# Silu on ScalarE with the router's weight as its scale, and one-hot vectors compared in one instruction

## The chip, the cores and the metric

One core of one Trainium2 chip runs the whole program. The metric is the device time of one execution in microseconds. Five engines work side by side and meet through semaphores: TensorE (PE, with its weight loads shown apart as PEld), VectorE (DVE), ScalarE (ACT), GpSimd (POOL) and SyncE (SP), which here only issues DMAs.

## The reference

The input `x` is 2 sequences of 2048 tokens with 256 channels. After a layer norm, a recurrent branch (RWKV-7 time mixing, 4 heads of 64) gives `s`, and a feed-forward branch gives `g`. The change is in the second branch and in where it meets the first:

```
logits = xn @ gate_w.T + gate_b                # 8 experts
scores = softmax(logits);  top_v, top_i = top_k(scores, 2)
val_sum = top_v.sum(-1)                        # the router's weight
for e in range(8):
    gate  = (top_i == e).sum(-1) * val_sum     # 0 or val_sum
    inter = xn @ wi.T + bi + (xn @ lora_A[e].T) @ lora_B[e].T
    out  += gate * (relu(inter) @ wo.T + bo)
g = silu(out)
x = x + s * g
```

Both chosen experts have the same weight `val_sum`. So `out` is `val_sum * y1`, where `y1` is the sum of the two experts' outputs, `(relu1 + relu2) @ wo.T + 2 * bo`.

## The kernel before

The work goes in 16 tiles of 128 tokens of each sequence (two chunks `g` of 64 tokens of each sequence, so 128 partitions times `G = 2`). A tile passes through three stages, and each of the 18 steps of the program (loop at L1495) works on three tiles at once: `front` of one tile (norm, router, mixing, projections), `rec` of the tile before it (the recurrence and the experts) and `post` of the tile before that (output projection, gate, residual). Step 1 has `front` alone, step 2 `front` and `rec`, steps 3 to 16 all three, step 17 `rec` and `post`, step 18 `post` alone.

The order on every engine is written out by hand in one function `tile` for each engine (PE L578, ACT L913, POOL L1056, DVE L1386). Each engine runs its list in order, and an instruction that waits for a semaphore holds up all that is behind it on that engine. `till(name, n)` gives the count to wait for. At the start of a step each engine waits for `act_end`, `pool_end` and `dve_end` of the step before; in the middle steps TensorE first does `base(0)`.

What the change touches:

- The router's one-hot vectors on VectorE: `first_expert` (L1172) and `second_expert` (L1185) end with one compare for each chunk, 128x8 each (L1183, L1195). `gate_sum` (L1205) leaves the router's weight in `vsum`, one number per token.
- The expert sum: `down` on TensorE (L275) adds into the bank `FB`; `y1_` (L1272) reads it on VectorE and adds the bias; `ypre` (L1277) multiplies by `vsum`, one instruction per chunk.
- The gate, one step later: `ysg_` on ScalarE (L850) takes Sigmoid of `y1`; `fgate_` on VectorE (L1282) multiplies the two; `o_read` (L1286) multiplies the output projection by `fgate`.

ScalarE evaluates its functions from a table, and a row ACT_TABLE_LOAD stands in its list wherever the next function needs another one. In the second half of a step its list runs: `kraw_` (two copies out of a bank, L819 and L820, once TensorE's `wk_B` is there), `sig_` (Sigmoid of the decay, L806), `copy_blocks` (four copies into `tinvT`, L872), `zt_e` (L848), `hg` (Tanh, L796), `inv_last` (L878), `p_out` (L883), `keys_out` (L887), `relu(2, 3)` (L762), `sa_out` (L893).

On TensorE the same stretch is `wk_B` (L360, L362), `inv_off(4)`, `rec_p(0)`, `top_x`, `zt_` (L289, the transposes of `zz`), `diff(3)` (L263), `g_A` (L337, waits for `sig_done`), `top_off` (L501), `keys_to_tokens(0)` (L510), `o_` (L300, waits for `hg_done`), `rec_sa(0)` (L542, waits for `p_done`). The bank that `keys_to_tokens(0)` writes is the one that `zt_e` reads, so TensorE waits there for ScalarE:

```
if post:
    pe.wait_ge(*till("zt_done", 1))
...
keys_to_tokens(0)
```

Of the kernel before, what the change touches and what calls it, by code (L numbers as in the profile page):

```python
# [28 lines left out]
G = 2  # L29
# [15 lines left out]
PER = dict(xn_done=G, xm_done=2, dx_done=3, mixt_done=2, miu_mm=3, sig_done=2, agate_done=2, xmask_done=2, e8_done=2 * G,  # L45
           oh1_done=G, oh2_done=G, dg2_done=2, v_done=3, down_mm=PAIRS, var_done=G, ypre_done=G,
           g_mm=LEVELS, g_stored=LEVELS, ar_scaled=LEVELS, bk0_scaled=LEVELS, bk1_scaled=LEVELS, tot_done=LEVELS,
# [7 lines left out]
       "y_done", "inc_mm", "dec_done", "state_done", "bkt_mm", "bkt_done", "yc_done", "ysq_done", "v8_done", "sd8_done",  # L55
       "bv_done", "bv_shifted", "yn_done", "zz_done", "down_mm", "y1_read", "ypre_done"}
REC |= {f"{n}_{p}_{e}" for n, e in (("z1", "mm"), ("z2", "mm"), ("relu1", "done"), ("relu2", "done"), ("hid", "done"))
        for p in range(PAIRS)}
POSTS = {"ysg_done", "fgate_done", "zt_mm", "zt_done", "o_mm", "o_read", "out_done", "out_stored"}
# [3 lines left out]
DOWN_ORDER = (1, 0, 2, 3)  # L63


def program(nc, x, par, weights, consts, out):
    ctx = ExitStack()
    with ctx:
# [60 lines left out]
        e2 = sb("e2", [128, G])  # L129
        vsum = [sb(f"vsum{i}", [128, G]) for i in range(2)]  # L130
        hit = sb("hit", [128, G, E])
# [10 lines left out]
        y1 = sb("y1", [128, G, C])  # L142
        ysg = sb("ysg", [128, G, C])
        fgate = sb("fgate", [128, G, C])
# [98 lines left out]
        def _(pe):  # L243
# [30 lines left out]

            def down(p):  # L275
                pe.wait_ge(*till(f"hid_{p}_done", 1))
                if p == DOWN_ORDER[0] and steps["rec"]:
                    pe.wait_ge(*till("y1_read", 0))
                for j in range(2):
                    for g in range(G):  # L280
                        last = mm(FB[:, g * C:(g + 1) * C], hid[:, p, j * 256 + g * L:j * 256 + (g + 1) * L],  # L281
                                  w["wo"][:, 2 * p + j, :], start=(p == DOWN_ORDER[0] and j == 0 and g == 0),
                                  stop=(p == DOWN_ORDER[-1] and j == 1), skip_group_check=True)
                last.then_inc(S("down_mm"), 1)
# [293 lines left out]
            def tile(step, front, rec, post):  # L578
# [30 lines left out]
                if rec:  # L609
                    diff(0)  # L610
                    down(1)
                    gram(2)
# [109 lines left out]
                if rec:  # L722
                    y_state(1)
                    rec_y(1)
                    rec_inc(1)
                    down(0)
                    down(2)
                    down(3)
                if front:
# [22 lines left out]
        def _(act):  # L752
# [364 lines left out]
        def _(dve):  # L1117
# [66 lines left out]

            def second_expert():  # L1185
                dve.wait_ge(*till("oh1_done", G))
                need(run(v.tensor_scalar(rest[:, :, :], oh1[:, :, :], -1.0, 1.0, ALU.mult, ALU.add)))
                for g in range(G):
                    t = run(v.scalar_tensor_tensor(hit[:, g, :], lg[:, g, :], top8[:, g, 1:2], rest[:, g, :],
                                                   ALU.is_ge, ALU.mult))  # L1190
                need(t)
                need(run(v.tensor_tensor(hit[:, :, :], hit[:, :, :], rev8[:].unsqueeze(1).to_broadcast([128, G, E]), ALU.mult)))
                need(run(v.tensor_reduce(hmx[:, :], hit[:, :, :], AX.X, ALU.max)))
                for g in range(G):
                    run(v.tensor_scalar(oh2[:, g, :], hit[:, g, :], hmx[:, g:g + 1], None, ALU.is_equal), "oh2_done")  # L1195

            def expert_masks():
                dve.wait_ge(*till("oh2_done", G))
                need(run(v.tensor_tensor(oh2[:, :, :], oh2[:, :, :], oh1[:, :, :], ALU.subtract)))
# [5 lines left out]
            def gate_sum():  # L1205
                dve.wait_ge(*till("e8_done", 2 * G))
                need(run(v.tensor_reduce(esum[:, :], e8[:, :, :], AX.X, ALU.add)))
                need(run(v.reciprocal(esum[:, :], esum[:, :])))
                need(run(v.scalar_tensor_tensor(vsum[steps["front"] % 2][:, :], e2[:, :], 1.0, esum[:, :], ALU.add, ALU.mult)))

# [60 lines left out]

            def y1_():  # L1272
                dve.wait_ge(*till("down_mm", PAIRS))
                run(v.scalar_tensor_tensor(y1[:, :, :], w["bo"][:].unsqueeze(1).to_broadcast([128, G, C]), 2.0,
                                           FB[:, :].rearrange("p (g n) -> p g n", g=G), ALU.mult, ALU.add), "y1_read")

            def ypre():  # L1277
                dve.wait_ge(*till("y1_read", 1))
                for g in range(G):
                    run(v.tensor_scalar(y1[:, g, :], y1[:, g, :], vsum[steps["rec"] % 2][:, g:g + 1], None, ALU.mult), "ypre_done")  # L1280

            def fgate_():  # L1282
                dve.wait_ge(*till("ysg_done", 1))
                run(v.tensor_tensor(fgate[:, :, :], y1[:, :, :], ysg[:, :, :], ALU.mult), "fgate_done")

            def o_read():  # L1286
                dve.wait_ge(*till("o_mm", 1))
                dve.wait_ge(*till("fgate_done", 1))
                if steps["post"]:
# [96 lines left out]
            def tile(step, front, rec, post):  # L1386
# [51 lines left out]
                if rec:  # L1438
# [31 lines left out]
                if rec:  # L1470
                    v8_()
                    y1_()
                if front:
                    bonus_e(rec)
                if rec:
                    ypre()
                    group_norm()
# [119 lines left out]
```

## Time and profile before

| | |
|---|---|
| median of 3 runs | 1081.84 us (1080.71 to 1085.01) |
| the profiled execution | 1081.82 us, of which the span is 1079.9 us |
| TensorE busy | 1035.7 us, 96% of the span |
| VectorE busy | 878.4 us, 81% |
| ScalarE busy | 627.8 us, 58% |
| GpSimd busy | 464.4 us, 43% |
| granted TensorE clock, mean | 0.985 |

Busy shares are means over the whole span. The steady steps, 3 to 16, are what counts: 14 of 18, some 64 us each. In the rows below, a time in front is the start in microseconds from the span's start, the next number how long the group took, "x4" how many instructions it holds, and a bracket at the end the idle time before it and what ended it. A matmul row of TensorE counts two hardware passes for one matmul of the program.

### The profile page before, as it was taken

The numbers are of one execution on the slowest core, as the hardware profiler recorded it, in microseconds if no ns is written. First come the engines' busy times: TensorE is split into PE (matmuls) and PEld (weight loads), VectorE is DVE, ScalarE is ACT, GpSimd is POOL, SyncE is SP. The second block draws the span as 40 slices with busy tenths as digits, with TensorE's granted clock in tenths as the row PEclk, the third lists the DMA queues.
The fourth block names the chain that finished last, engine by engine and source line by source line (L and its number), as shares of the span: only waits on it lengthen the run. The fifth ranks groups of instructions, "written<-read, shape, count | busy, mean of one in ns | idle before, by whom it ended". The sixth has DMA issues, their size and how long they took to land.

```text
span 1079.9 us, 42650 instructions
## 1 busy us (share of the span) xinstructions
PE 1035.7 (96%) x18530; PEld 823.1 (76%) x18530; DVE 878.4 (81%) x1738; ACT 627.8 (58%) x1433; POOL 464.4 (43%) x541
## 2 busy tenths in 40 slices
PE   4699999999999999999999999999999999999985
PEld 3487778778787777878778787878878787787764
DVE  3488888888888888888888888888888888888753
ACT  2456555566665566566565656556656655666552
POOL 3145262534536254352625435262452625345331
PEclk8799999999999999999999999999999999999997
DMA  7000000000000000000000000000000000000000
GB/s 236 1 12 4 1 4 21 3 22 2 23 2 3 21 4 21 2 23 2 4 21 3 22 2 5 20 3 22 2 22 2 4 21 4 21 3 13 1 4 20
DMA packets 9256, 16.95 MB, mean 16 GB/s; under 512 B 1904, under 2 KB 3824, under 8 KB 8816
## 3 DMA queue, kind: packets, MB, share of 16 engines
q1 hardware_dynamic: 9072, 14.23, 4.0%
q8 instruction: 148, 2.42, 1.0%
q14 instruction: 36, 0.29, 0.1%
HBM read 10.03 MB, written 4.19 MB: 13 GB/s over the span
## 4 chain that ended last, share of the span: by engine, by line
PE 94%; ACT 2%; issue 2%; DVE 2%; SPq 0%; DMA 0%; POOLq 0%; POOL 0%; DVEq 0%
PE bank L263 11%; PE bank L257 11%; PE bank L281 10%; PE grams L451 10%; PE bank L330 5%; PE bank L377 3%; PE bank L320 3%; PE bank L392 3%; PE bank L384 3%; PE bank L300 2%; PE bank L466 2%; PE bank L477 2%; PE grams L542 2%; PE grams L531 2%; PE grams L519 2%
## 5 line engine op out<-in xcount | busy, mean ns | idle before, releaser
L1021 POOL TENSOR_TENSOR bk<-bk,tot 128x256 f32<-128x256 f32 x192 | 161.4, 857 | 184.8 <-PE grams L451 184.8
L864 ACT ACTIVATE gl<-gm 32x128 f32<-32x128 f32 x320 | 98.8, 309 | 152.5 <-DVE gm L1302 146.7
L1302 DVE COPY_PREDICATED gm<-c_mask_g,grams 128x1024 f32<-128x1024 int32 x96 | 159.9, 1666 | 1.8 <-PE grams L451 0.7
L1002 POOL TENSOR_TENSOR xd<-mtmp,xnc 128x512 f32<-128x512 f32 x96 | 127.5, 1336 | 59.9 <-DVE mtmp L1168 59.9
L762 ACT ACTIVATE relu<-bank,prm 128x256 f32<-128x256 f32 x256 | 105.5, 471 | 56.3 <-PE bank L263 54.6
L263 PE MATMUL bank<-xmt,w_lora_B 128*128 128x256 f32 x512 | 134.2, 390 | 0.1
L257 PE MATMUL bank<-xnc,w_wi 128*128 128x256 f32 x512 | 122.0, 386 | 4.2 <-ACT scratch L988 4.2
L281 PE MATMUL bank<-w_wo,hid 128*128 128x256 f32 x512 | 117.4, 382 | 0.0
L451 PEld LDWEIGHTS grams<-ar,bk 64*64 64x64 f32 x6144 | 98.9, 134 | 21.4 <-issue 13.4
L451 PE MATMUL grams<-ar,bk 64*64 64x64 f32 x6144 | 112.3, 221 | 1.5 <-DVE gm L1302 1.4
L257 PEld LDWEIGHTS bank<-xnc,w_wi 128*128 128x128 f32 x512 | 93.4, 190 | 21.8 <-issue 6.7
L1312 DVE TENSOR_TENSOR ar<-ar,tot 128x512 f32<-128x512 f32 x96 | 89.3, 931 | 21.6 <-PE grams L451 19.8
L281 PEld LDWEIGHTS bank<-w_wo,hid 128*128 128x128 f32 x512 | 96.0, 190 | 13.5
L263 PEld LDWEIGHTS bank<-xmt,w_lora_B 128*128 128x128 f32 x512 | 90.7, 190 | 17.2 <-issue 5.8
L1168 DVE SCALAR_TENSOR_TENSOR mtmp<-bank,prm,dx 128x256 f32<-128x256 f32 x192 | 80.3, 473 | 16.3 <-PE bank L330 14.3
L1062 POOL TENSOR_TENSOR scratchp<-eps 128x1 f32<-128x1 f32 x18 | 3.5, 193 | 194.7 <-ACT scratch L988 181.3
L1052 POOL TENSOR_TENSOR bk<-kh,rootd 128x512 f32<-128x512 f32 x16 | 20.2, 1265 | 96.5 <-DVE kh L1227 96.5
L330 PE MATMUL bank<-mixt,w_x_B 32*128 32x256 f32 x384 | 56.2, 411 | 3.2 <-DVE mtmp L1168 1.8
L1033 POOL TENSOR_TENSOR out_t<-out_t,x_in 128x512 f32<-128x512 f32 x16 | 20.3, 1269 | 63.9 <-DVE out_t L1291 63.9
L831 ACT ACTIVATE zb<-bank 64x512 f32<-64x512 f32 x32 | 18.9, 592 | 48.8 <-PE bank L392 48.4
L1270 DVE TENSOR_TENSOR hid<-relu 128x512 f32<-128x512 f32 x64 | 43.8, 685 | 3.3 <-ACT relu L762 2.7
L1234 DVE SCALAR_TENSOR_TENSOR dg<-rr,prm,kh 128x256 f32<-128x256 f32 x32 | 42.4, 1364 | 1.7
(180 smaller groups left out, 2175.6 us busy)
## 6 DMA issues: line engine op xcount, KB each, us to landing
x_in<-x SPq DMA_DIRECT2D x16, 256.0 KB, 2.7
out<-out_t SPq DMA_DIRECT2D x16, 256.0 KB, 2.0
w_wi<-w_wi_dram SPq DMA_DIRECT2D x1, 1024.0 KB, 6.6
w_wo<-w_wo_dram SPq DMA_DIRECT2D x1, 1024.0 KB, 8.9
w_lora_B<-w_lora_B_dram SPq DMA_DIRECT2D x1, 512.0 KB, 8.6
w_x_A<-w_x_A_dram SPq DMA_DIRECT2D x1, 256.0 KB, 2.7
w_x_B<-w_x_B_dram SPq DMA_DIRECT2D x1, 256.0 KB, 2.9
w_kW<-w_kW_dram SPq DMA_DIRECT2D x1, 256.0 KB, 3.4
```

Of the source, the lines that this page charges most:

```text
L257: mm(ZB[p % 2][:, j * 256:(j + 1) * 256], w["wi"][:, c, f:f + 128], xnc[steps["rec"] % 2][:, c, :], start=(j == 0 and c == 0), stop=False, ...
L263: last = mm(ZB[p % 2][:, j * 256:(j + 1) * 256], w["lora_B"][:, f:f + 128], xmt[steps["rec"] % 2][:, e, :], start=False, stop=True, skip_g ...
L281: last = mm(FB[:, g * C:(g + 1) * C], hid[:, p, j * 256 + g * L:j * 256 + (g + 1) * L], w["wo"][:, 2 * p + j, :], start=(p == DOWN_ORDER[0 ...
L330: last = mm(MIU[k % 2][:, c * 256:(c + 1) * 256], w["x_B"][o:o + 32, u, c * 128:(c + 1) * 128], mixt[o:o + 32, u, :], start=True, stop=True)
L451: last = mm(dst, bk[o:o + 64, g, c, 1 - b, k, :], rhs, start=True, stop=True)
L762: A(dst[:, p % 2, j * 256:(j + 1) * 256], ZB[p % 2][:, j * 256:(j + 1) * 256], ACT.Relu, bias=prm[:, P_BI + 2 * p + j:P_BI + 2 * p + j + 1 ...
L864: A(gl[l % 2][o:o + 32, :, :, :].rearrange("p q g (c n m) -> p (q g c) n m", c=2, m=m), right(gm[o:o + 32, :, :, :, b, 0, 32 * k:32 * k + ...
L1002: tt(xd[:, q, :, :], mtmp[:, k % 2, :, :], xnc[steps["front"] % 2][:, :, :], ALU.add).then_inc(S(f"xd_{k}_done"), 1)
L1021: tt(v, v, d, ALU.mult).then_inc(S(f"bk{k}_scaled"), 1)
L1168: run(v.scalar_tensor_tensor(mtmp[:, k % 2, c, :], MIU[k % 2][:, c * 256:(c + 1) * 256], prm[:, P_LAM + 2 * q + c:P_LAM + 2 * q + c + 1], ...
L1302: run(v.copy_predicated(dst, msk.to_broadcast([128, 32, HALF // m, m]), src), "g_stored")
L1312: run(v.tensor_tensor(a, a, tv[:, :, 0].unsqueeze(1).unsqueeze(3).to_broadcast([128, 2, 4 * n, m]), ALU.mult), "ar_scaled")
```

## The change

ScalarE now computes `fgate = Silu(vsum * y1)` in two instructions, one per chunk, with the router's weight as the per-partition scale. `ypre` and `fgate_` on VectorE are gone, and so is the tile `ysg`. Since the weight is now read a step later, `vsum` has three buffers in place of two. `y1_` gets a wait for `fgate_done` (the Silu of the tile before must have read `y1`). The two one-hot compares per expert become one `tensor_tensor` of 128x16 with the maximum broadcast. `DOWN_ORDER` is replaced by the arguments `first` and `final`; the order of the matmuls stays as it was.

```diff
             def ysg_():
-                act.wait_ge(*till("ypre_done", 0))
-                A(ysg[:, :, :], y1[:, :, :], ACT.Sigmoid).then_inc(S("ysg_done"), 1)
+                act.wait_ge(*till("y1_read", 0))
+                for g in range(G):
+                    A(fgate[:, g, :], y1[:, g, :], ACT.Silu, scale=vsum[steps["post"] % 3][:, g:g + 1]).then_inc(S("fgate_done"), 1)
...
-                for g in range(G):
-                    run(v.tensor_scalar(oh1[:, g, :], hit[:, g, :], hmx[:, g:g + 1], None, ALU.is_equal), "oh1_done")
+                run(v.tensor_tensor(oh1[:, :, :], hit[:, :, :], hmx[:, :].unsqueeze(2).to_broadcast([128, G, E]), ALU.is_equal), "oh1_done")
...
-            def y1_():
+            def y1_(post):
                 dve.wait_ge(*till("down_mm", PAIRS))
+                if post:
+                    dve.wait_ge(*till("fgate_done", G))
                 run(v.scalar_tensor_tensor(y1[:, :, :], w["bo"][:].unsqueeze(1).to_broadcast([128, G, C]), 2.0,
                                            FB[:, :].rearrange("p (g n) -> p g n", g=G), ALU.mult, ALU.add), "y1_read")
 
-            def ypre():
-                dve.wait_ge(*till("y1_read", 1))
-                for g in range(G):
-                    run(v.tensor_scalar(y1[:, g, :], y1[:, g, :], vsum[steps["rec"] % 2][:, g:g + 1], None, ALU.mult), "ypre_done")
-
-            def fgate_():
-                dve.wait_ge(*till("ysg_done", 1))
-                run(v.tensor_tensor(fgate[:, :, :], y1[:, :, :], ysg[:, :, :], ALU.mult), "fgate_done")
...
-                if post:
-                    fgate_()
                 if front:
                     decay_step(rec)
```

TensorE, GpSimd and SyncE have the same instructions, waits and order as before. The first place where the lists differ beyond names is ScalarE in steps 3 to 16, from the gate's function to `copy_blocks`. Before (`ysg` is the gate's Sigmoid, `h_wk` a Tanh, `sig` the decay's Sigmoid; `gl`, `relu`, `kraw` and `tinvT` are copies, a Relu and such):

```order
L852 ACT_TABLE_LOAD
L852 ACTIVATE ysg<-y 128x512
L864 ACTIVATE gl<-gm 32x128 x4
L762 ACTIVATE relu<-bank,prm 128x256 x2
L788 ACTIVATE h_wk<-bank 128x256
L864 ACTIVATE gl<-gm 32x128 x4
L762 ACTIVATE relu<-bank,prm 128x256 x4
L819 ACTIVATE kraw<-bank 128x512
L820 ACTIVATE ksq<-bank 128x512
L806 ACTIVATE sig<-bank,prm 128x2x128 x2
L872 ACTIVATE tinvT<-blocks 32x8x32 x4
```

and now:

```order
L851 ACT_TABLE_LOAD
L851 ACTIVATE fgate<-y,vsum 128x256 x2
L863 ACTIVATE gl<-gm 32x128 x4
L760 ACTIVATE relu<-bank,prm 128x256 x2
L786 ACTIVATE h_wk<-bank 128x256
L863 ACTIVATE gl<-gm 32x128 x4
L760 ACTIVATE relu<-bank,prm 128x256 x4
L817 ACTIVATE kraw<-bank 128x512
L818 ACTIVATE ksq<-bank 128x512
L804 ACT_TABLE_LOAD
L804 ACTIVATE sig<-bank,prm 128x2x128 x2
L871 ACTIVATE tinvT<-blocks 32x8x32 x4
```

A table load now stands between `ksq` and `sig`: 14 of them in all, one in each of the steps 3 to 16. The load ahead of the gate's function (L852 before, L851 now) is there in both.

VectorE, steps 3 to 16, halfway through the step (`x_top` is the top block of the inverse, `tot` the decay, `hid` the hidden layer, `oh` the one-hot vectors):

```order
L1346 COPY x_top<-bank 128x256
L1284 TENSOR_TENSOR fgate<-y,ysg 128x512
L1217 TENSOR_SCALAR tot<-sig 128x512
L1270 TENSOR_TENSOR hid<-relu 128x512
L1187 TENSOR_SCALAR rest<-oh 128x16
L1189 SCALAR_TENSOR_TENSOR hit<-lg,top,rest 128x8 x2
L1192 TENSOR_TENSOR hit<-hit,c_rev 128x16
L1193 TENSOR_REDUCE hmx<-hit 128x2
L1195 TENSOR_SCALAR oh<-hit,hmx 128x8 x2
```

and now:

```order
L1336 COPY x_top<-bank 128x256
L1214 TENSOR_SCALAR tot<-sig 128x512
L1267 TENSOR_TENSOR hid<-relu 128x512
L1185 TENSOR_SCALAR rest<-oh 128x16
L1187 SCALAR_TENSOR_TENSOR hit<-lg,top,rest 128x8 x2
L1190 TENSOR_TENSOR hit<-hit,c_rev 128x16
L1191 TENSOR_REDUCE hmx<-hit 128x2
L1192 TENSOR_TENSOR oh<-hit,hmx 128x16
```

The product `fgate` is gone, so `tot` is next behind `x_top`, and one compare of 128x16 stands where two of 128x8 stood. Near the end of such a step, before:

```order
L1367 TENSOR_REDUCE v<-ysq 128x8
L1274 SCALAR_TENSOR_TENSOR y<-w_bo,bank 128x512
L1265 STREAM_TRANSPOSE bonus<-bank 128x128
L1280 TENSOR_SCALAR y<-y,vsum 128x256 x2
L1371 RECIPROCAL rs<-sd 128x8
```

and now:

```order
L1357 TENSOR_REDUCE v<-ysq 128x8
L1273 SCALAR_TENSOR_TENSOR y<-w_bo,bank 128x512
L1262 STREAM_TRANSPOSE bonus<-bank 128x128
L1361 RECIPROCAL rs<-sd 128x8
```

The pair that multiplied `y` by `vsum` is gone between `bonus` and `rs`.

## Rows read from the trace of the kernel before

**Rows 1.** The page's chain of waits, shares of the span by engine.

```profile
PE 94%; ACT 2%; issue 2%; DVE 2%; SPq 0%; DMA 0%; POOLq 0%; POOL 0%; DVEq 0%
```

**Rows 2.** Busy time by engine in one steady step (us, instructions, clock).

```profile
582.00:645.50 63.50, 63.50 (x1160) 50.82 (x1159) 55.30 (x109) 38.77 (x89) 28.82 (x33) 1.00 0.04 11
```

**Rows 3.** Timeline, steady step, ScalarE: start, us, engine, line, operation [idle <- releaser].

```profile
600.00 0.60 ACT L819 ACTIVATE kraw<-bank 128x512 f32<-128x512 f32 x1 [2.26 <-PE bank L362]
...
600.97 0.84 ACT L806 ACTIVATE sig<-bank,prm 128x256 f32<-128x256 f32 x2
601.68 1.71 ACT L872 ACTIVATE tinvT<-blocks 32x256 f32<-32x256 f32 x4
603.42 0.60 ACT L848 ACTIVATE zt<-bank 128x512 f32<-128x512 f32 x1
```

**Rows 4.** Timeline, the same step, TensorE's matmuls.

```profile
599.58 0.38 PE L362 MATMUL bank<-h_wk,w_wk_B 64*128 64x256 f32 x1
...
603.45 1.03 PE L337 MATMUL bank<-xd,w_g_A 128*128 128x256 f32 x4
...
605.03 0.65 PE L510 MATMUL bank<-c_ident,bk 128*128 128x128 f32 x4
605.52 1.89 PE L300 MATMUL bank<-w_oW,zt 128*128 128x256 f32 x8
607.35 0.68 PE L542 MATMUL grams<-pp,tinvT 64*64 64x64 f32 x16
```

**Rows 5.** Timeline, second step, ScalarE, the same place.

```profile
89.66 0.60 ACT L819 ACTIVATE kraw<-bank 128x512 f32<-128x512 f32 x1 [2.26 <-PE bank L362]
90.15 0.59 ACT L820 ACTIVATE ksq<-bank 128x512 f32<-128x512 f32 x1
90.76 1.28 ACT L806 ACT_TABLE_LOAD   x1
92.05 0.84 ACT L806 ACTIVATE sig<-bank,prm 128x256 f32<-128x256 f32 x2
92.78 1.71 ACT L872 ACTIVATE tinvT<-blocks 32x256 f32<-32x256 f32 x4
94.52 0.38 ACT L796 ACTIVATE h_g<-bank 128x256 f32<-128x256 f32 x1
...
95.58 0.38 ACT L883 ACTIVATE pp<-grams 128x256 f32<-128x256 f32 x1
```

**Rows 6.** Timeline, second step, TensorE.

```profile
92.95 1.13 PE L337 MATMUL bank<-xd,w_g_A 128*128 128x256 f32 x4
...
96.11 0.68 PE L542 MATMUL grams<-pp,tinvT 64*64 64x64 f32 x16 [0.82 <-ACT pp L883]
```

**Rows 7.** Timeline, steady step, ScalarE, the gate's sigmoid and what follows.

```profile
587.45 0.63 ACT L852 ACTIVATE ysg<-y 128x512 f32<-128x512 f32 x1
588.98 1.30 ACT L864 ACTIVATE gl<-gm 32x128 f32<-32x128 f32 x4 [0.90 <-DVE gm L1302]
```

**Rows 8.** Timeline, steady step, VectorE.

```profile
602.55 1.05 DVE L1284 TENSOR_TENSOR fgate<-y,ysg 128x512 f32<-128x512 f32 x1
...
606.55 0.36 DVE L1195 TENSOR_SCALAR oh<-hit,hmx 128x8 f32<-128x8 f32 x2
...
623.22 0.69 DVE L1274 SCALAR_TENSOR_TENSOR y<-w_bo,bank 128x512 f32<-128x512 f32 x1 [1.05 <-PE bank L281]
```

**Rows 9.** Timeline, last two steps: VectorE, ScalarE, TensorE.

```profile
1065.29 0.61 DVE L1280 TENSOR_SCALAR y<-y,vsum 128x256 f32<-128x256 f32 x2
...
1071.01 0.58 ACT L848 ACTIVATE zt<-bank 128x512 f32<-128x512 f32 x1
1071.65 3.78 PE L300 MATMUL bank<-w_oW,zt 128*128 128x256 f32 x8 [1.36 <-ACT zt L848]
```

**Rows 10.** Timeline: TensorE one step later, ScalarE in step 16.

```profile
658.62 0.25 PE L477 MATMUL bank<-xb,turned 32*32 32x32 f32 x4 [0.71 <-issue]
...
983.47 0.60 ACT L819 ACTIVATE kraw<-bank 128x512 f32<-128x512 f32 x1 [2.55 <-PE bank L362]
```

More of the change, by code:

```diff
@@ L45 @@
 PER = dict(xn_done=G, xm_done=2, dx_done=3, mixt_done=2, miu_mm=3, sig_done=2, agate_done=2, xmask_done=2, e8_done=2 * G,
-           oh1_done=G, oh2_done=G, dg2_done=2, v_done=3, down_mm=PAIRS, var_done=G, ypre_done=G,
+            dg2_done=2, v_done=3, down_mm=PAIRS, var_done=G, fgate_done=G,
            g_mm=LEVELS, g_stored=LEVELS, ar_scaled=LEVELS, bk0_scaled=LEVELS, bk1_scaled=LEVELS, tot_done=LEVELS,
@@ L129, in program @@
         e2 = sb("e2", [128, G])
-        vsum = [sb(f"vsum{i}", [128, G]) for i in range(2)]
+        vsum = [sb(f"vsum{i}", [128, G]) for i in range(3)]
         hit = sb("hit", [128, G, E])
@@ L273, in diff, with down @@
                 from_experts(p, 1).then_inc(S(f"z2_{p}_mm"), 1)
-            def down(p):
+            def down(p, first=False, final=False):
                 pe.wait_ge(*till(f"hid_{p}_done", 1))
-                if p == DOWN_ORDER[0] and steps["rec"]:
+                if first and steps["rec"]:
                     pe.wait_ge(*till("y1_read", 0))
@@ L281, in down @@
                         last = mm(FB[:, g * C:(g + 1) * C], hid[:, p, j * 256 + g * L:j * 256 + (g + 1) * L],
-                                  w["wo"][:, 2 * p + j, :], start=(p == DOWN_ORDER[0] and j == 0 and g == 0),
-                                  stop=(p == DOWN_ORDER[-1] and j == 1), skip_group_check=True)
+                                  w["wo"][:, 2 * p + j, :], start=(first and j == 0 and g == 0),
+                                  stop=(final and j == 1), skip_group_check=True)
                 last.then_inc(S("down_mm"), 1)
@@ L610, in tile @@
                     diff(0)
-                    down(1)
+                    down(1, first=True)
                     gram(2)
@@ L727, in tile @@
                     down(2)
-                    down(3)
+                    down(3, final=True)
                 if front:
@@ L1193, in second_expert @@
                 need(run(v.tensor_reduce(hmx[:, :], hit[:, :, :], AX.X, ALU.max)))
-                for g in range(G):
-                    run(v.tensor_scalar(oh2[:, g, :], hit[:, g, :], hmx[:, g:g + 1], None, ALU.is_equal), "oh2_done")
+                run(v.tensor_tensor(oh2[:, :, :], hit[:, :, :], hmx[:, :].unsqueeze(2).to_broadcast([128, G, E]), ALU.is_equal), "oh2_done")
             def expert_masks():
-                dve.wait_ge(*till("oh2_done", G))
+                dve.wait_ge(*till("oh2_done", 1))
                 need(run(v.tensor_tensor(oh2[:, :, :], oh2[:, :, :], oh1[:, :, :], ALU.subtract)))
@@ L1208, in gate_sum @@
                 need(run(v.reciprocal(esum[:, :], esum[:, :])))
-                need(run(v.scalar_tensor_tensor(vsum[steps["front"] % 2][:, :], e2[:, :], 1.0, esum[:, :], ALU.add, ALU.mult)))
+                need(run(v.scalar_tensor_tensor(vsum[steps["front"] % 3][:, :], e2[:, :], 1.0, esum[:, :], ALU.add, ALU.mult)))
             def decay_step(rec):
@@ L1270, in hidden @@
                 run(v.tensor_tensor(hid[:, p, :], relu1[:, p % 2, :], relu2[:, p % 2, :], ALU.add), f"hid_{p}_done")
-            def y1_():
+            def y1_(post):
                 dve.wait_ge(*till("down_mm", PAIRS))
+                if post:
+                    dve.wait_ge(*till("fgate_done", G))
                 run(v.scalar_tensor_tensor(y1[:, :, :], w["bo"][:].unsqueeze(1).to_broadcast([128, G, C]), 2.0,
                                            FB[:, :].rearrange("p (g n) -> p g n", g=G), ALU.mult, ALU.add), "y1_read")
-            def ypre():
-                dve.wait_ge(*till("y1_read", 1))
-                for g in range(G):
-                    run(v.tensor_scalar(y1[:, g, :], y1[:, g, :], vsum[steps["rec"] % 2][:, g:g + 1], None, ALU.mult), "ypre_done")
-            def fgate_():
-                dve.wait_ge(*till("ysg_done", 1))
-                run(v.tensor_tensor(fgate[:, :, :], y1[:, :, :], ysg[:, :, :], ALU.mult), "fgate_done")
             def o_read():
                 dve.wait_ge(*till("o_mm", 1))
-                dve.wait_ge(*till("fgate_done", 1))
+                dve.wait_ge(*till("fgate_done", G))
                 if steps["post"]:
```

11 lines of the change are left out of this document (4 added, 7 removed).

## The prediction

> **What bounds the kernel now.** I read the chain of waits first: 94% of the time to the last instruction is TensorE's own work [rows 1]. Then the busy times of one middle step: TensorE is busy 63.50 of 63.50 us at full clock, VectorE 55.30, ScalarE 38.77, GpSimd 28.82 [rows 2]. In the steady steps nothing makes TensorE wait, so work taken off another engine brings nothing there by itself, and an added wait of TensorE is not made up for later: whatever it loses is added to the step. The question is therefore not how much VectorE is relieved but where TensorE's list has the least slack against ScalarE's, since ScalarE gets work. For that I laid the timelines of ScalarE and TensorE beside each other for the stretch between `wk_B` and `rec_sa(0)` [rows 3, 4]. Last I looked for a step in which ScalarE already has the instruction that the change adds; step 2 is one [rows 5, 6].
>
> **What the change takes from VectorE.** Per steady step: the product `fgate`, 1.05 us [rows 8]; the pair that multiplies by `vsum`, two instructions that take 0.61 us together [rows 9]; and for each expert a pair of compares of 0.36 us becomes one instruction [rows 8]. The new compare reads twice the elements of one old one. Its cost lies between nothing saved (0.36) and half (0.18); I take half, 0.4 us a step for both experts. Sum: 1.05 + 0.61 + 0.36, about 2.0 us a step less of 55.30. In time it is worth nothing there: VectorE waits 1.05 us for TensorE ahead of `y1` as it is [rows 8], and TensorE waits for nobody. Nor can it cost anything: the new compare would have to be longer than the pair by more than the idle time ahead of `y1`, and nothing else is added there.
>
> **What it gives ScalarE in the first half of the step.** The Sigmoid over 128x512 took 0.63 us [rows 7]. Two instructions over 128x256 with a per-partition operand take 0.84 us together in `sig` [rows 3], so Silu costs 0.2 us more. No row shows Silu. If it took the time of Sigmoid, 0.2; if twice that, 0.84 + 0.2 = about 1.0. Behind it `pack_gram(3)` (the copies `gl`) stood idle 0.90 us for VectorE [rows 7]: the first is wholly hidden, the second comes 0.1 us out of it, into copies that run well ahead of their matmuls. I take nothing, with 0.1 us a step as the other end. The table load ahead of it was there before. The new wait of `y1` for `fgate_done` stands ahead of `y1` at 623 us, the Silu would be done at about 588 us [rows 7, 8]: over 30 us of slack, and behind it `bonus` and the group norm are not touched. Silu itself waits for `y1` of the step before, long done.
>
> **What it gives ScalarE in the second half: one more table load.** The function table that serves Silu and the `h_wk` Tanh does not serve `sig`, so a load stands between `ksq` and `sig` in steps 3 to 16. Step 2 of the kernel before has this very sequence: `ksq` from 90.15, load 90.76 to 92.04, `sig` 92.05, `tinvT` 92.78 [rows 5]. From the start of `kraw` to the start of `tinvT` it takes 92.78 - 89.66 = 3.12 us; without the load 601.68 - 600.00 = 1.68 us [rows 3]. The load pushes what is behind it by 1.44 us: 1.28 of its own and the rest because two functions in a row overlap and a load doesn't overlap.
>
> ScalarE's idle time of 2.26 us ahead of `kraw` [rows 3] doesn't hide it, since the load stands behind `kraw` and `ksq`, which wait for TensorE's `wk_B` (last matmul 599.58 + 0.38 = 599.96) [rows 4]. What is queued behind it, with TensorE's needs:
> - `sig` ends at 601.81 before, 603.25 now. `g_A` waits for it and starts at 603.45 [rows 4]. In step 2 it started 0.06 us after `sig` (92.89, 92.95) [rows 5, 6]; that gives 603.31 here. It is just in time; if its weights are late by some 0.1, this is swallowed by the next point, which waits longer.
> - `zt` ends at 603.42 + 0.60 = 604.02 before [rows 3], 605.46 now. `keys_to_tokens(0)` (L510) waits for it and started at 605.03 [rows 4]. From the end of `zt` to the start of the waiting matmul there are 0.06 us in step 18 (1071.59 and 1071.65) [rows 9]. So it starts at 605.52: **0.49 us late**. Slack was 0.95, the push is 1.44.
> - `h_g` is next: 0.10 before the end of `zt`, 605.36 to 605.74. `o_` waits for it and would start at 605.52 + 0.49 = 606.01. No further wait.
> - `tinvT` (0.77) and `pp`: in step 2 `pp` starts 1.06 us after `h_g` and takes 0.38 [rows 5], so it ends at 606.80. `rec_sa(0)` comes at 607.35 + 0.49 = 607.84 [rows 4]. In step 2, where `o_` with its 1.8 us is missing, the same push made TensorE wait 0.82 us for `pp` [rows 6]: the mechanism is seen there already.
> - From `sa_out` on ScalarE waits for TensorE again, and the lag is gone. The rest of the step is later by 0.49 us as a whole, with the old slacks.
>
> On VectorE, `tot` waits for `sig` (603.25) and started at 603.60 less a small overlap, behind the product that is now gone [rows 8]; it is not late.
>
> **What the skill says of it.** The row of the load is 1.28 us, with nothing but 0.02 us on either side [rows 5]. The Trainium skill, page "ScalarE: Activation LUTs", section "What ACT_TABLE_LOAD costs", states 1283 ns for the load and about 1380 ns of drain, 2.66 us for every switch; its "Rules for kernel authors" say to group functions by table set, which speaks against this change. The load's length agrees; the drain is not seen in step 2. By the page's figure each stall would be 1.38 us longer, which gives an estimate of 1107 us; the last rival below is that case.
>
> **The sum.** 14 steps (3 to 16) by 0.49 = 6.9 us. Step 2 and step 17 have no added load (17 has no `sig`). At the end the change gives something: from the last `y1` on, VectorE's list is on the path, and the pair of 0.61 us goes [rows 9]. In step 18 the function stands directly ahead of `zt`, which TensorE waits for (1.36 us [rows 9]), and Silu's pair takes 0.21 more there; this leaves 0.4 us gained. In all 6.9 - 0.4 = +6.5 us on the profiled execution's 1081.82 (span 1079.9 and 1.9 around it), which is the median of the runs, 1081.84, within 0.02. **Forecast 1088.3 us, +0.6%.** The bounds of the steady term: 0.44 us (0.05 for how well slack and push can be read) and 0.7 (L510's weight load no longer hidden, 0.1, and 0.1 for Silu in the first half), so 6.2 to 9.8 for 14 steps, and a time of 1087.6 to 1091.2. With the scatter of a median of few runs, whose runs here lie 1.1 below and 3.2 above it, its own range is 1087.0 to 1090.5.
>
> **Rivals.**
> - *Not slower, because the stall is paid from gaps that are there anyway.* Steps are not all 63.50 us long: from `kraw` at 600.00 to that at 983.47 six steps take 383.47, 2.5 us more than 6 x 63.50 [rows 3, 10]. The gaps are inside the runs of small matmuls, as the 0.71 us ahead of four of the `inv_off` matmuls at 658.62, and end by "issue", with no engine waited for [rows 10]. If they come from TensorE's supply of instructions (an assumption, no row names it), a stop of 0.49 us could let it catch up. At 0.41 a step they hold 5.7 us over 14 steps; all of them recovered leaves 1081.8 + 6.5 - 5.7 = 1082.6, half of them 1085.4. Against it: L510 stands at 605.03 [rows 4], the next gap at 658.62, 54 us and most of a step's matmuls behind it. Decisive is whether a stop so far ahead still helps. 12%.
> - *Not slower, because the load is hidden*: if ScalarE gets ahead by more than 0.5 us between `kraw` and `zt`, so that the stall does not show. What could be faster is only the four copies `tinvT` (1.71 us together), with VectorE idle beside them instead of in the product. Nothing in step 2 shows it, where VectorE had no product either and they took the same 1.71. Then only the end counts: 1081.4. 5%.
> - *Faster by over 0.5%* needs 0.4 us a step off TensorE's own list, through less VectorE traffic beside it; TensorE is at full clock with no waits [rows 2]. 14 x 0.4 and the 0.4 at the end would give 1081.8 - 6.0 = 1075.8. The mechanism would be matmuls or weight loads that become shorter when VectorE reads less; nothing in the rows speaks for it, and `keys_to_tokens` took 0.65 us with VectorE busy beside it [rows 4]. 3%.
> - *Slower still*: `g_A` and L510 both lose the overlap of their weight loads. In step 2 `g_A` took 1.13 where the unhindered one took 1.03 [rows 4, 6]. Between 0.6 and 0.75 a step: 1081.8 + 14 x 0.68 - 0.4 = 1090.9. 8%.
> - *The switch costs the load's length twice* (ScalarE idle for another 1.28 us beside Silu's or `sig`'s table): the stall is 1.77 a step, 1081.8 + 24.8 - 0.4 = 1106. Step 2 speaks against it. 2%.
>
> **The numbers.** The forecast's case holds 70%. What a measurement of this kernel can tell from no change is about 0.5%, 5.4 us, so the line to "slower" lies at 1087.2, just below the forecast; 0.11 of the forecast's own case falls under it, and the two cases of no loss. Slower 0.59 + 0.08 + 0.02 = 0.69; same 0.11 + 0.12 + 0.05 = 0.28; faster 0.03. Range 1084.8 to 1091.0: it leaves out the hidden load, the faster case, the doubled switch, and some of the largest recovery, under 2 in 10 together.
>
> **What would show it.** In the profile after: a row ACT_TABLE_LOAD of 1.28 us between `ksq` and `sig` in 14 steps; L510 with an idle time of about 0.5 us ended by ScalarE's `zt`, 14 times, near 6.9 us in all; `g_A` at most 0.1 late; `gl` behind Silu still waiting for VectorE; VectorE's busy time 27 to 33 us less and no gain from it; the final L300 0.4 us closer to the last `y1`. Wrong, if L510 waits under 0.3 us, if TensorE waits for `pp` or `sig` more than for `zt`, or if the "issue" gaps are fewer.

## The result, and the profile after

| | before | changed |
|---|---|---|
| median | 1081.79 us (10 runs, 1079.37 to 1085.01) | 1088.75 us (10 runs, 1085.76 to 1092.45) |
| ratio | | 1.0059, 95% interval 1.0045 to 1.0074 |
| the profiled execution | 1081.82 us, span 1079.9 | 1089.39 us, span 1087.5 |
| shortest steady step, `kraw` to `kraw` | 63.49 us | 63.98 us |

The forecast was 1088.3 us, with a chance of 0.69 for slower by over 0.5%. The changed kernel is slower by 0.6% (0.45 to 0.74% by the interval).

The page of the changed kernel, busy time, share of the span and instructions of each engine, and the chain of waits:

```profile
PE 1037.3 (95%) x18530; PEld 823.7 (76%) x18530; DVE 849.5 (78%) x1658; ACT 648.7 (60%) x1463; POOL 458.1 (42%) x541
...
PE 87%; ACT 9%; issue 2%; DVE 1%; SPq 0%; POOL 0%; DMA 0%; POOLq 0%; DVEq 0%
```

TensorE and GpSimd have the same instructions as before. VectorE has 28.9 us less (878.4 to 849.5), ScalarE 20.9 us more (627.8 to 648.7). The chain of waits, which ran over TensorE for 94% of the span [rows 1], now runs over ScalarE for 9%, where it was 2%: that is about 5 us more in each steady step. What TensorE waited for, from the list of its waits (us in total, times, longest):

```profile
PE bank L508 <- ACT zt L846: 5.8, 14, 0.4
...
PE bank L335 <- ACT sig L804: 3.3, 1, 3.3
```

The first row is new: 14 waits for `zt`, all of one length. The second is the one of step 1 and was there before. ScalarE in one steady step, the place of [rows 3]:

```profile
601.57 0.60 ACT L817 ACTIVATE kraw<-bank 128x512 f32<-128x512 f32 x1 [2.27 <-PE bank L360]
602.06 0.59 ACT L818 ACTIVATE ksq<-bank 128x512 f32<-128x512 f32 x1
602.67 1.28 ACT L804 ACT_TABLE_LOAD   x1
603.97 0.84 ACT L804 ACTIVATE sig<-bank,prm 128x256 f32<-128x256 f32 x2
604.70 1.71 ACT L871 ACTIVATE tinvT<-blocks 32x256 f32<-32x256 f32 x4
606.43 0.60 ACT L846 ACTIVATE zt<-bank 128x512 f32<-128x512 f32 x1
606.93 0.38 ACT L794 ACTIVATE h_g<-bank 128x256 f32<-128x256 f32 x1
```

The load runs from 602.67 to 603.95, between the end of `ksq` and the start of `sig`. From the start of `kraw` to that of `tinvT` it is 3.13 us, as in step 2 of the kernel before [rows 5], against 1.68. TensorE in the same stretch, for [rows 4]:

```profile
605.02 1.03 PE L335 MATMUL bank<-xd,w_g_A 128*128 128x256 f32 x4
605.97 0.69 PE L499 MATMUL bank<-blocks,x_top 32*32 32x32 f32 x32
607.08 0.66 PE L508 MATMUL bank<-c_ident,bk 128*128 128x128 f32 x4 [0.42 <-ACT zt L846]
607.58 1.89 PE L298 MATMUL bank<-w_oW,zt 128*128 128x256 f32 x8
609.40 0.68 PE L540 MATMUL grams<-pp,tinvT 64*64 64x64 f32 x16
```

`g_A` (L335) is as far behind `kraw` as before (3.45 us), L508 (which was L510) is 5.51 us behind it and not 5.03: 0.48 us late. The row shows 0.42 of idle time, the rest is the overlap with the matmul before it. L298 and L540 follow at their old distances, with no further wait. On VectorE, the place of [rows 8]:

```profile
604.84 1.28 DVE L1214 TENSOR_SCALAR tot<-sig 128x512 f32<-128x512 f32 x1 [0.64 <-ACT sig L804]
...
607.65 0.18 DVE L1192 TENSOR_TENSOR oh<-hit,hmx 128x16 f32<-128x16 f32 x1
```

`tot` now waits for `sig`, since the product ahead of it is gone, and the merged compare takes 0.18 us. The Silu of all steps, from the list of groups (busy, mean ns of one | idle before):

```profile
L851 ACT ACTIVATE fgate<-y,vsum 128x256 f32<-128x256 f32 x32 | 14.5, 501 | 0.2
```

501 ns each, 0.91 for the pair, where 0.84 was taken. The end of the program, the place of [rows 9], first VectorE, then ScalarE and TensorE:

```profile
1072.73 0.69 DVE L1273 SCALAR_TENSOR_TENSOR y<-w_bo,bank 128x512 f32<-128x512 f32 x1 [1.97 <-PE bank L279]
```

```profile
1078.00 0.91 ACT L851 ACTIVATE fgate<-y,vsum 128x256 f32<-128x256 f32 x2
1078.81 0.57 ACT L846 ACTIVATE zt<-bank 128x512 f32<-128x512 f32 x1
```

```profile
1079.44 3.56 PE L298 MATMUL bank<-w_oW,zt 128*128 128x256 f32 x8 [1.63 <-ACT zt L846]
```

From the last `y` to the start of the last projection it is 6.71 us; before it was 7.08, from 1064.57 to 1071.65.

The two spans differ by 7.6 us. Four parts make it up. Up to the first stop, in step 3, the changed run was 1.1 us ahead (`kraw` of step 3 at 152.75 and 153.86); this is scatter, for the first `kraw` of the program starts anywhere from 32.4 to 35.2 us in the thirteen profiles of this document. From `kraw` of step 3 to that of step 16 it took 835.39 us against 829.61, +5.8, which is 13 stops of 0.48 less 0.5 us of other gaps. The stop of step 16 is another 0.5. Step 17 and the end make up the last 2.4, and no stop of the change lies there. In the middle of step 17 TensorE's granted clock fell: counted from the first matmul of the step, L499 is at 34.93 us in the kernel before and at 37.93 in the changed one, 3.0 later. The wait ahead of step 18 became 0.6 shorter (4.03 us for 4.67), since the pair that multiplied `y` is gone. The same stretch of the changed kernel and of the one before (us, busy time of PE, PEld, DVE, ACT, POOL, granted clock):

```profile
1045.00:1050.00 5.00, 4.47 (x132) 3.29 (x132) 1.49 (x4) 2.51 (x7) 3.82 (x5) 0.66 0.03 7
1050.00:1056.00 6.00, 4.80 (x66) 4.00 (x68) 2.81 (x6) 2.25 (x5) 0.00 (x0) 0.72 0.00 0
```

```profile
1040.00:1045.00 5.00, 3.47 (x140) 2.65 (x139) 3.03 (x7) 2.36 (x7) 3.65 (x5) 1.00 0.03 7
1045.00:1051.00 6.00, 6.00 (x112) 4.88 (x110) 1.93 (x5) 4.65 (x11) 0.00 (x0) 1.00 0.01 3
```

The first two rows are the changed kernel, at 0.66 and 0.72 of full clock (means over stretches partly at 2.4 and partly at 1.2 GHz). In the run of before the stretch stands at 1.00 and the clock fell later, for step 18; over the whole span both have 0.985. The profiles below show the fall in step 17 with and without the change.

### The profile page after: what moved, and what is told of

It is laid out like the page before. It is cut to its first block, busy times and chain, and to the rows that moved or that the text cites. A ratio compares the mean times of both kernels' runs of the same rounds, so it can differ in the third digit from the quotient of the medians.

```text
span 1087.5 us, 42615 instructions
## 1 busy us (share of the span) xinstructions
PE 1037.3 (95%) x18530; PEld 823.7 (76%) x18530; DVE 849.5 (78%) x1658; ACT 648.7 (60%) x1463; POOL 458.1 (42%) x541
## 4 chain that ended last, share of the span: by engine, by line
PE 87%; ACT 9%; issue 2%; DVE 1%; SPq 0%; POOL 0%; DMA 0%; POOLq 0%; DVEq 0%
PE bank L255 11%; PE bank L279 10%; PE bank L261 10%; PE grams L449 10%; PE bank L328 5%; PE bank L375 3%; PE bank L318 3%; PE bank L390 3%; PE bank L382 3%; PE bank L298 2%; PE bank L464 2%; ACT tinvT L871 2%; ACT L804 2%; PE grams L540 2%; PE bank L475 2%
## 5 line engine op out<-in xcount | busy, mean ns | idle before, releaser
L1001 POOL TENSOR_TENSOR xd<-mtmp,xnc 128x512 f32<-128x512 f32 x96 | 121.2, 1270 | 58.7 <-DVE mtmp L1167 58.7
L760 ACT ACTIVATE relu<-bank,prm 128x256 f32<-128x256 f32 x256 | 105.6, 471 | 56.3 <-PE bank L261 54.6
L261 PEld LDWEIGHTS bank<-xmt,w_lora_B 128*128 128x128 f32 x512 | 91.4, 191 | 17.4 <-issue 5.8
```

What stands on the lines that cost most here:

```text
L261: last = mm(ZB[p % 2][:, j * 256:(j + 1) * 256], w["lora_B"][:, f:f + 128], xmt[steps["rec"] % 2][:, e, :], start=False, stop=True, skip_g ...
L760: A(dst[:, p % 2, j * 256:(j + 1) * 256], ZB[p % 2][:, j * 256:(j + 1) * 256], ACT.Relu, bias=prm[:, P_BI + 2 * p + j:P_BI + 2 * p + j + 1 ...
L1001: tt(xd[:, q, :, :], mtmp[:, k % 2, :, :], xnc[steps["front"] % 2][:, :, :], ALU.add).then_inc(S(f"xd_{k}_done"), 1)
```

## The experiments

### The load alone, without Silu's work and with VectorE as it was

```diff
                 if post:
                     ysg_()
+                    if front:
+                        A(scratch[:, 1:2], eps[:, 0:1], ACT.Silu)
```

> The kernel before, with one Silu over a single column (of a scratch tile) behind the gate's Sigmoid in steps 3 to 16. It forces a load for Silu there and a second load between ksq and sig, and leaves VectorE's list as it was. Theory (the load between ksq and sig makes the output transposes of the keys wait for zt): idle time ahead of L510 ended by zt in 14 steps, 0.42 each in the row as in the changed kernel (0.48 from matmul to matmul), nothing from the extra load in the first half (1.5 us against 0.9 us of idle time and 2 us of slack behind it): +6.7 us, 1088.5. Rival (the two products and the compares taken from VectorE make up for part of the cost, so the load alone costs more): stalls at L510 over 0.5 us, or +8 us and more. Rival (the table is not what matters, the Silu itself is): no stall at L510, 1081.8.

Ratio to the kernel before 1.0071 (1.0047 to 1.0096), median 1090.1. The row of TensorE's waits:

```profile
PE bank L510 <- ACT zt L848: 5.8, 14, 0.4
```

The same 14 waits of the same length as in the changed kernel, and the shortest step is again 63.97 to 63.99 us. The load between `ksq` and `sig` is enough for the whole loss of the steady steps, with VectorE's list as it was. The extra load in the first half was hidden.

### The same number of loads, one of them early

```diff
                 if front:
+                    if post:
+                        A(scratch[:, 0:1], eps[:, 0:1], ACT.Sigmoid)
                     kraw_()
                     sig_()
```

> The changed kernel, with one Sigmoid over a single column ahead of kraw in steps 3 to 16, where ScalarE stands idle 2.3 us for TensorE. The number of loads is the same as in the changed kernel, only their place differs. Theory (the place of the load decides): the load ends before wk_B is done, no idle time ahead of L508, steps back to 63.5 us plus the gaps of issue; the end is 0.4 us shorter: 1081.4, -0.7% against the changed kernel. Rival (the number of switches counts, or Silu and its scale cost elsewhere): 1087 to 1089 as before.

Ratio 0.9995 (0.9979 to 1.0010). ScalarE, then TensorE:

```profile
595.92 1.28 ACT L955 ACT_TABLE_LOAD   x1
597.21 0.20 ACT L955 ACTIVATE scratch<-eps 128x1 f32<-128x1 f32 x1
598.15 0.60 ACT L817 ACTIVATE kraw<-bank 128x512 f32<-128x512 f32 x1 [0.74 <-PE bank L360]
...
601.57 0.60 ACT L846 ACTIVATE zt<-bank 128x512 f32<-128x512 f32 x1
```

```profile
603.18 0.66 PE L508 MATMUL bank<-c_ident,bk 128*128 128x128 f32 x4
```

The load and the one-column Sigmoid fill part of the time in which ScalarE waits for `wk_B`; 0.74 us of that wait is left. L508 stands 5.03 us behind `kraw`, without a wait, and the steps are back at 63.49. ScalarE does 0.2 us a step more than in the changed kernel and the time is 0.6% lower. So the number of table switches isn't the cost, their place is. What VectorE has less brings nothing that can be measured. It is also less than the list of removed instructions says: its busy time is 856.0 us, 22.4 below the kernel before and not 28.9, since without the product `hid` runs beside a product on GpSimd and takes 1.75 us where it took 0.68 in the changed kernel:

```profile
601.16 1.45 POOL L1003 TENSOR_TENSOR xd<-mtmp,xnc 128x512 f32<-128x512 f32 x1
601.40 1.75 DVE L1269 TENSOR_TENSOR hid<-relu 128x512 f32<-128x512 f32 x1
```

### The merged compares alone, and VectorE's relief alone

```diff
-                for g in range(G):
-                    run(v.tensor_scalar(oh1[:, g, :], hit[:, g, :], hmx[:, g:g + 1], None, ALU.is_equal), "oh1_done")
+                run(v.tensor_tensor(oh1[:, :, :], hit[:, :, :], hmx[:, :].unsqueeze(2).to_broadcast([128, G, E]), ALU.is_equal), "oh1_done")
...
```

> The kernel before, with the one-hot compares merged and nothing else. Theory: 0.56 us less on VectorE in a step (2 x (0.46 to 0.18) by the two profiles), nothing on TensorE, 1081.8, within 1 us. Rival (VectorE's time is worth something): up to 0.5 us a step, 1075 to 1080.

```diff
             def ysg_():
-                act.wait_ge(*till("ypre_done", 0))
-                A(ysg[:, :, :], y1[:, :, :], ACT.Sigmoid).then_inc(S("ysg_done"), 1)
+                act.wait_ge(*till("y1_read", 0))
+                A(fgate[:, :, :], y1[:, :, :], ACT.Sigmoid).then_inc(S("fgate_done"), 1)
...
-                if post:
-                    fgate_()
...
-                    ypre()
```

> The kernel before, without the multiplication by the router's weight and without the product of y1 and its Sigmoid: the gate is the bare Sigmoid of the expert sum, so the gate's part of the result is left out. VectorE has 1.7 us less a step, ScalarE the same loads as before. Theory: TensorE's list does not move, only the end gets 0.6 us shorter (the pair behind the last y1): 1081.2. Rival (VectorE's relief shortens POOL's copies or TensorE's steps): below 1079.

The second kernel leaves out both products, the one by the router's weight and the one of `y1` and its Sigmoid, so its gate has another value. Ratios 1.0007 (0.9989 to 1.0025) and 1.0000 (0.9985 to 1.0014). Both are where the theory has them, within what can be told, with 5.6 and 17.4 us less busy time on VectorE (0.4 and 1.2 us a step where 0.56 and 1.7 were expected). The 0.6 us at the end of the second one is too small for the interval, but its profile has it: 6.43 us from the last `y` to the last projection, against 7.08.

### zt ahead of the four copies

```diff
-                if rec:
-                    copy_blocks()
                 if post:
                     zt_e()
+                if rec:
+                    copy_blocks()
```

> The changed kernel, with the copy zt ahead of the four copies into tinvT; the load stays between ksq and sig. Theory (TensorE waits for whatever ScalarE finishes last of what it needs, and the sum of ScalarE's work ahead of o_ is the same): the wait at L508 goes, since zt ends 3.7 us after the start of kraw and is needed at 5.0; h_g now ends at 5.75 and o_ (L298) was due at 5.52, so a new wait of about 0.3 us for h_g stands there in 14 steps. Against the kernel before: 14 x 0.3 - 0.4 = +3.8, 1085.6 on a base of 1081.8. Rival (only the copy zt matters): no wait in the second half, 1081.4. Rival (the load itself stops TensorE or memory): wait at L508 as in the changed kernel, 1088.3.

Ratio 1.0042 (1.0025 to 1.0058). ScalarE, TensorE's matmuls, and its weight loads:

```profile
605.98 0.60 ACT L846 ACTIVATE zt<-bank 128x512 f32<-128x512 f32 x1
606.46 1.72 ACT L871 ACTIVATE tinvT<-blocks 32x256 f32<-32x256 f32 x4
608.20 0.38 ACT L794 ACTIVATE h_g<-bank 128x256 f32<-128x256 f32 x1
```

```profile
607.89 0.66 PE L508 MATMUL bank<-c_ident,bk 128*128 128x128 f32 x4
608.64 1.99 PE L298 MATMUL bank<-w_oW,zt 128*128 128x256 f32 x8
```

```profile
608.63 1.59 PEld L298 LDWEIGHTS bank<-w_oW,zt 128*128 128x128 f32 x8 [0.33 <-ACT h_g L794]
```

The wait at L508 is gone and another stands at L298, for `h_g`. From L508 to L298 there are 0.75 us, 0.49 before, and the projection takes 1.99 where it took 1.89 [rows 4]: its first weight load no longer runs beside the matmuls ahead of it. Together 0.36, and the shortest steps are 63.84 to 63.87. The theory had 0.3 and forgot that 0.1; it is the extra that the prediction named for `g_A` and L510, here at L298. The rival by which only `zt` matters is out, and so is the one by which the load itself stops TensorE, since nothing waits at L508 any more.

### The copies split around h_g

```diff
-                if rec:
-                    copy_blocks()
                 if post:
                     zt_e()
+                if rec:
+                    copy_blocks((0, 32))
                 if front:
                     hg()
                 if rec:
+                    copy_blocks((64, 96))
                     inv_last()
```

> The changed kernel, with ScalarE's order zt, two copies into tinvT, h_g, the other two copies; number and place of the table loads as in the changed kernel. Theory (it is slack and not the load): zt needed at 5.0 us after kraw ends at 3.7, h_g needed at 5.5 ends at about 5.0, pp needed at 7.35 ends at 6.8: no wait of TensorE at all, steps at 63.5 plus gaps, 1081.4, as with the early table. Rival (a load in this place costs whatever the order): 0.3 to 0.5 us a step, 1085.6 to 1088.3.

Ratio 1.0017 (1.0002 to 1.0032). TensorE in a steady step, then in step 2, and the busy times of step 2 behind it:

```profile
606.08 0.66 PE L508 MATMUL bank<-c_ident,bk 128*128 128x128 f32 x4
606.57 1.89 PE L298 MATMUL bank<-w_oW,zt 128*128 128x256 f32 x8
608.39 0.68 PE L540 MATMUL grams<-pp,tinvT 64*64 64x64 f32 x16
```

```profile
96.59 0.68 PE L540 MATMUL grams<-pp,tinvT 64*64 64x64 f32 x16 [1.43 <-ACT pp L882]
```

```profile
95.00:100.00 5.00, 3.57 (x32) 2.00 (x30) 2.03 (x11) 4.31 (x11) 0.00 (x0) 0.75 0.01 3
100.00:106.00 6.00, 6.00 (x86) 4.88 (x85) 4.50 (x7) 3.17 (x6) 0.34 (x1) 0.93 0.01 1
```

In the steady steps the theory holds: no wait, steps of 63.49 to 63.50, with the load still between `ksq` and `sig`. So the load costs by the slack it meets and not by being there. The time is 0.2% above what was expected, and in the profile as much comes from step 2: it is 66.38 us where 64.20 were, since `pp` comes 0.6 us later there (1.43 against 0.82 [rows 6]) and the clock fell behind the wait (0.75, then 0.93 of full).

### Two loads in the same place, and a second profile of it

```diff
                     kraw_()
+                    if post:
+                        A(scratch[:, 0:1], eps[:, 0:1], ACT.Sqrt)
                     sig_()
```

> The changed kernel, with one Sqrt over a single column between ksq and sig in steps 3 to 16, so that two loads stand there. Theory (slack is used up, from here every nanosecond counts): push 1.44 + 1.28 + 0.24 = 2.96 us, slack 0.95, TensorE late by 2.0 us a step, of which 1.37 show at g_A (L335) as a wait for sig and 0.64 at L508 as a wait for zt: 14 x 2.0 - 0.4 = +27.7, 1109.5. Rival (a switch costs its load and as much again): 3.5 us and more a step, over 1130. Rival (TensorE makes up for waits out of its issue gaps): under 1.8 us a step, below 1107.

Ratio 1.0323 (1.0304 to 1.0341), median 1118.58. TensorE's waits:

```profile
PE bank L335 <- ACT sig L804: 19.8, 15, 3.3
PE bank L508 <- ACT zt L846: 6.6, 14, 0.5
```

Less the 3.3 us of step 1 these are 16.5 us at L335 in 14 waits, 1.18 each, and 0.47 each at L508. The shortest step is 65.48 us, 2.0 above the kernel before: the push of 2.96 less 0.95 of slack. (The idle times of 1.65 us leave out what was overlap before, as above.) A switch therefore costs its load and nothing as long again. But the time is above the 1109.5 that was worked out: by 9 us, or by 7 if the ratio is put on the same base of 1081.8. Of the five runs the profiled one was the fastest, 1112.72, with a mean granted clock of 0.984; the others had 1118.5 to 1121.6 and 0.976 to 0.980. A second profile was to show where that goes.

> The kernel with two loads once more, for a second profile: its timed runs (1118.5 to 1121.6) lay 6 to 9 us above its profiled one (1112.7) and had a lower granted clock (0.976 to 0.980 against 0.984). Theory (the longer stops of TensorE, 1.2 us and 0.5 us on end, are now and then followed by some microseconds at half clock, as once in that profile, in the step of 67.16 us): if the time is near 1118, four or so steps of 67 us and the rest at 65.5. Rival (the stalls themselves are longer in those runs): all steps longer than 65.5, granted clock full in them.

1115.61 us, granted clock 0.980. Of its 13 steps from the third on nine lie between 65.48 and 66.33 us, four are 67.1 to 67.8. In the first of these, TensorE and the busy times (granted clock behind POOL's):

```profile
288.35 1.13 PE L335 MATMUL bank<-xd,w_g_A 128*128 128x256 f32 x4 [1.18 <-ACT sig L804]
...
290.57 1.11 PE L508 MATMUL bank<-c_ident,bk 128*128 128x128 f32 x4 [0.47 <-ACT zt L846]
291.48 3.12 PE L298 MATMUL bank<-w_oW,zt 128*128 128x256 f32 x8
```

```profile
289.00:294.00 5.00, 4.53 (x45) 3.59 (x44) 1.32 (x7) 4.05 (x11) 0.00 (x0) 0.66 0.02 5
294.00:297.00 3.00, 3.00 (x39) 1.87 (x39) 2.33 (x4) 1.45 (x4) 1.27 (x1) 1.00 0.00 0
```

Behind the two stops the projection takes 3.12 us where it took 1.89, at 0.66 of full clock over 5 us, and then the clock is full again. That costs 1.6 us, on top of the two waits. The waits themselves are as long as in the first profile (1.18 and 0.47, shortest step 65.48), so the rival by which they are longer is out. The theory was right about the waits and lacked a second cost, which comes in some steps and not in others: four in this profile (each with a fall of the clock), one in the first. How many there were in the unprofiled runs is not known; their lower mean clock fits with more of them.

### Early table and a shorter end, and the early table in every step

To the kernel with the early table this adds, for step 18:

```diff
+                if post and not rec:
+                    zt_e()
                 if post:
                     ysg_()
...
-                if post:
+                if post and rec:
                     zt_e()
```

> The changed kernel with the early Sigmoid, and in step 18 the copy zt ahead of the Silu. Theory: steady steps as in the run with the early table; in step 18 L298 waits for zt 1.0 us less, since the load and the Silu run beside TensorE's matmuls; 1080.4, 1.3 us below the kernel before, which is less than the interval will tell. Rival (Silu is then late for the last product on VectorE): the end as before, 1081.4.

Ratio 0.9983 (0.9972 to 0.9993). The wait at the last projection:

```profile
PE bank L298 <- ACT zt L846: 0.7, 1, 0.7
```

0.7 us, 1.6 in the changed kernel. From the last `y` to the last projection it is 5.75 us, 6.71 there and 7.08 in the kernel before. For the next one the `if post` ahead of the early Sigmoid is left out.

> The changed kernel, with the one-column Sigmoid ahead of kraw in steps 1 and 2 as well, and zt ahead of the Silu in step 18. Theory: in step 1 g_A waits 1.3 us less for sig (the load runs while ScalarE waits for wk_B), in step 2 the wait of 0.82 us for pp goes, in step 18 1.0 us goes; steady steps at 63.5 plus gaps. 2.1 us less than the kernel with the early table and the other end (0.9983 of before), so 0.996 to 0.997 of the kernel before. Rival (steps 1 and 2 are held by something else just behind): no less than 0.998.

Ratio 0.9984 (0.9970 to 0.9998), median 1080.08 against 1082.08. Its waits:

```profile
PE bank L335 <- ACT sig L804: 1.9, 1, 1.9
...
PE grams L540 <- ACT pp L882: 0.8, 1, 0.8
```

`g_A` in step 1 waits 1.4 us less, but from `kraw` of step 1 to that of step 2 only 0.4 is left of it (55.54 us against 55.95 in the changed kernel): TensorE then waits longer for what comes next (2.48 us for `dg`, 1.96 in the changed kernel, among others). In step 2 the wait for `pp` did not go. This is a miss, and it corrects the prediction too, which had read the 0.82 us in step 2 as the work of the load. Without the load it is 0.78. It is the way from `top_off` over `inv_last` to `pp`, for which step 2 has no projection on TensorE as a cover: there ScalarE waits 0.25 us for `top_off` (L499), `inv_last` takes 0.77 and `pp` 0.38. Step 2 is 0.4 us shorter even so (63.84 against 64.21), by `g_A`. The rival, no less than 0.998, is what came. The steady steps had nothing to give, and the ratio is that of the version before it. Both versions are below the two kernels that were compared, about 0.75% below the changed one and 0.2% below the one before, the latter just clear of their intervals. By the profiles what they gain over the kernel before lies in the end (1.3 us) and, in the second, in the first two steps; the order in step 18 and the early table in steps 1 and 2 need no Silu, but they were not run on the kernel before.

### The changed kernel once more

> The changed kernel once more, for a second profile: how much of the difference of two profiles is the fixed part (14 stops of 0.48 us) and how much moves from run to run (gaps of issue, the half clock in step 17). Theory: shortest steps again 63.98, idle 0.41 or 0.42 ahead of L508 14 times; the start, the gaps and step 17 differ by up to 3 us. Rival (the half clock in step 17 belongs to the change): it is there again.

1088.72 us. The fixed part is the same to 0.01: 14 waits of 0.41 or 0.42 for `zt`, shortest step 63.98. The rest moved. From the first matmul of step 17 to that of step 18, with the pair of products still in the list: 56.3 us in the kernel before, 56.2 with the load alone, 59.0 with the merged compares alone. Without the pair: 55.5 with the early table, 57.8 and 58.7 in the two profiles of the changed kernel, 60.3 without the products. The fall of the clock behind these differences does not take the change: it stands in both of its profiles, but also in those of the merged compares alone and of the relief alone, and not in that of the early table, which has the whole change. Of all thirteen profiles ten have it in step 17: eight of the nine with the whole change and two of the other four. So the profiles don't tell whether the change makes it more frequent, nor what decides whether a run has it.

## Why the prediction was right

- *VectorE's relief is worth nothing.* Right: 28.9 us less busy time (27 to 33 were foreseen), and ratios of 1.0000 and 1.0007 with parts of it alone, 17.4 and 5.6 us less. The sum by removed instructions met it partly by chance: with the early table, where only the place of the load differs, the same list gives 22.4.
- *Silu in the first half is hidden.* Right; the pair takes 0.91 us and not the 0.84 of equal cost, and it made no difference: `gl` behind it still waits 0.62 us for VectorE, and with the load alone, without the pair, the steps are as long.
- *The load pushes by 1.44 us, of which 0.95 is slack.* This is the step on which the forecast rests. 0.49 was worked out, 0.48 measured in each of 14 steps. It came from a step of the old trace in which the instruction stood in the same place already, which is why it was so near.
- *No further wait behind it.* Right. `g_A` was on time, `h_g` and `pp` as well. How little room there is, the reordered kernel showed: with `zt` first, `h_g` is 0.3 late.
- *The end gives 0.4 back.* 0.37 by the profile.
- *The page's price of a switch.* The Trainium skill, page "ScalarE: Activation LUTs", section "What ACT_TABLE_LOAD costs": the load's 1283 ns is confirmed by every row, the drain of 1380 ns beside it is not; the second load added 1.28 and its companion instruction (steps of 65.48 us for 63.98, 1.50 more). The estimate by the page's figure, given as 1107 us, is 1107.6 by its own terms.
- *The gaps of issue make up for it.* The rival fell. From `kraw` of step 3 to that of step 16, the time above 13 shortest steps was 4.3 us in the kernel before, 3.7 and 3.2 in the two profiles of the changed one, 4.5 with the load alone, 3.9 with the early table, 3.5 with the merged compares alone. One sign of being wrong, fewer gaps, thus shows in the two profiles of the changed kernel, but within what they vary by themselves: kernels without the stops have 2.9 to 4.5, those with single stops 3.2 to 4.5. The gaps also keep their place: from `kraw` of step 7, 10 and 14 to the next one there are 0.4 to 1.5 us above the shortest step in each of the eleven profiles with single stops or none.
- *Wrong in detail*: the 0.82 us of step 2 was taken as proof that the load causes waits there. It causes 0.3 at `g_A` in that step; the wait for `pp` is there without it, 0.78 long.

The sum was 6.5 us, the medians differ by 7.0, the ratio gives 6.4 with 4.9 to 8.0. That the two profiles differ by 7.6 is no better or worse a match: 2.4 of it is step 17 and the end, and -1.1 the start, which no term of the sum had. What the profiles confirm term by term are the 14 stops and the 0.4 at the end.

## What to carry to other kernels

Where the engine that bounds a kernel has no idle time, as in the steady steps here, work taken from another engine brought nothing, and a merged or fused instruction should be judged by what it does to the tightest hand-over instead. Merging a function on ScalarE can split a run that shared one table; look in the instruction list for loads that appear somewhere else than at the edit, and compare their length with the slack of what is queued behind. The load was free where the engine waited for another anyway, and a one-column call of the function put it there; a new order of the instructions behind it hid it as well, without moving it.

## What was not expected

- A stop of TensorE can be followed by a cost beyond its length: behind waits of 1.18 and 0.47 us within 2.2 us, the granted clock fell to 0.66 over the next 5 us in some steps and not in others of the same run (67.1 and 65.5 us). Behind single stops of 0.42 us the granted clock stayed at 1.00 in all steady steps, in three profiles (two of the changed kernel, one of the load alone) with 14 stops each.
- Step 17, where TensorE waits often, took from 55.5 to 60.3 us in the profiles named above, and what makes it long is this fall of the clock, whichever kernel it was. (0.6 of the 4.8 us is the pair of products, which some of these kernels have and others not.) Of the 7.6 us between the two profiles 2.4 come from there.
- The product `fgate` on VectorE took 1.05 us in the steady steps and 0.69 in step 18, at 1071.14, where GpSimd was idle; in the steady step `bk` and `xd` ran on GpSimd beside it, from 601.85 to 604.72. It was costlier in the place where it stood, and even so nothing came of its removal; in the kernel with the early table `hid` took the place beside `xd` and became 1.07 longer.
